# Two of four probability tiles joined on GpSimd at the end of each batch of layer 0

## The reference, cut to what matters

```python
scores2 = jnp.einsum('bqh,bkh->bqk', Q_sub, K_char) * scale
sub2char = jnp.einsum('bqk,bkh->bqh', jax.nn.softmax(scores2, axis=-1), V_char)
sub2char = sub2char[:, lo] * (1 - w) + sub2char[:, hi] * w
gate = jax.nn.sigmoid(jnp.einsum('blh,oh->blo', jnp.concatenate([char2sub, sub2char], -1), Wg) + bg)
x = x + tanh(g_xattn[0]) * (gate * char2sub + (1 - gate) * sub2char)
```

## Time and profile before

| | |
|---|---|
| time of the kernel before | 1392.84 us, median of 3 runs, 1389.47 to 1395.42 |
| span of the profiled execution | 1388.3 us |
| TensorE busy in it | 1323.2 us, 95% |
| VectorE busy | 779.2 us, 56% |
| ScalarE busy | 736.2 us, 53% |
| GpSimd busy | 478.3 us, 34% |
| the gate of batches 0 to 3 ends at | 118.7, 210.8, 302.4 and 392.2 us |

### The profile page before, as it was taken

One profiled execution on the slowest core, in us unless ns is written; L12 is line 12 of the kernel. 1 busy time (PEld: TensorE's weight loads), 2 busy tenths in 40 slices (PEclk: granted clock), 3 DMA queues, 4 the chain that ended last, 5 costly groups with the idle time before them and its releaser, 6 DMA issues. The chain is left out here.

```text
span 1388.3 us, 25467 instructions
## 1 busy us (share of the span) xinstructions
PE 1323.2 (95%) x9828; PEld 1239.0 (89%) x9828; DVE 779.2 (56%) x1736; ACT 736.2 (53%) x1405; POOL 478.3 (34%) x378
## 2 busy tenths in 40 slices
PE   6999999999989999999999998899999999999996
PEld 5987969969759999999998998899999879999996
DVE  6566686776865535435444323666876774466322
ACT  4464555455554655555555554454554546567544
POOL 0100001001026656556465443111201246667544
PEclk9999999999999999999999999999999999999999
DMA  6102031220235545455363334112312166565322
GB/s 225 61 12 92 16 128 46 67 86 7 84 85 159 123 83 148 93 116 146 63 150 54 56 59 88 46 59 70 128 35 92 47 219 159 131 163 127 53 52 40
DMA packets 73675, 127.48 MB, mean 92 GB/s; under 512 B 7952, under 2 KB 53664, under 8 KB 73504
## 3 DMA queue, kind: packets, MB, share of 16 engines
q1 hardware_dynamic: 46816, 81.92, 17.9%
q0 software_dynamic: 26688, 43.34, 16.9%
HBM read 100.44 MB, written 24.79 MB: 90 GB/s over the span
## 5 line engine op out<-in xcount | busy, mean ns | idle before, releaser
L2551 DVE TENSOR_TENSOR m_hidden_lo<-m_act_out,m_hidden_hi 128x512 fp32r<-128x512 f32 x224 | 154.9, 693 | 353.6 <-ACT m_hidden_hi L2491 343.2
L434 PE MATMUL banks<-m_down_hi,m_hidden_hi 128*128 128x256 f32 x896 | 258.5, 288 | 1.4 <-DVE m_hidden_lo L2551 0.9
L434 PE MATMUL banks<-m_down_lo,m_hidden_hi 128*128 128x256 f32 x896 | 255.8, 286 | 2.4 <-issue 2.4
L434 PE MATMUL banks<-m_down_hi,m_hidden_lo 128*128 128x256 f32 x896 | 255.8, 285 | 0.0
L434 PE MATMUL banks<-m_xt_hi,m_up_hi 128*128 128x256 f32 x640 | 184.1, 288 | 1.4 <-DVE m_xt_lo L2534 1.4
L434 PE MATMUL banks<-m_xt_hi,m_up_lo 128*128 128x256 f32 x640 | 180.8, 282 | 0.0
L434 PE MATMUL banks<-m_xt_lo,m_up_hi 128*128 128x256 f32 x640 | 180.6, 282 | 0.0
L434 PEld LDWEIGHTS banks<-m_down_hi,m_hidden_hi 128*128 128x128 f32 x896 | 172.2, 192 | 4.6 <-DVE m_hidden_lo L2551 1.1
L434 PEld LDWEIGHTS banks<-m_down_lo,m_hidden_hi 128*128 128x128 f32 x896 | 172.2, 192 | 2.6 <-issue 2.6
L434 PEld LDWEIGHTS banks<-m_down_hi,m_hidden_lo 128*128 128x128 f32 x896 | 172.0, 192 | 0.0
L2491 ACT ACTIVATE m_hidden_hi<-m_act_out 128x512 fp32r<-128x512 f32 x224 | 141.6, 632 | 7.1
(11 more groups left out here) (387 smaller groups left out, 3430.5 us busy)
## 6 DMA issues: line engine op xcount, KB each, us to landing
stage<-in_up SPq DMA_DIRECT2D x22, 512.0 KB, 5.0
stage<-in_down SPq DMA_DIRECT2D x21, 512.0 KB, 4.0
stage<-in_ctx_rows SPq DMA_DIRECT2D x20, 512.0 KB, 4.3
stage<-in_ctx_cols SPq DMA_DIRECT2D x24, 402.0 KB, 3.3
m_stage<-in_down SPq DMA_DIRECT2D x10, 512.0 KB, 5.2
m_stage<-in_up SPq DMA_DIRECT2D x9, 512.0 KB, 4.8
rows<-xn SPq DMA_DIRECT2D x8, 528.0 KB, 3.7
stage<-in_ctx_picked SPq DMA_DIRECT2D x8, 512.0 KB, 4.6
```

The source lines that it names most:

```text
L434: mm = q.e.matmul(dst, a, b, start=first and n == 0, stop=last and n == 2, skip_group_check=True)
L2551: q.e.tensor_tensor(lo, m.act[(n * HP + h) % ACTS], f32(hi), ALU.subtract).then_inc(*hidden_lo.mark((layer, n, h)))
```

## The change

- **Joins.** Tiles 0 and 1 are joined on GpSimd (`gpsimd_back_finish`): a multiplication of the upper probabilities in place with their weight, and an addition into `a0.pc`. Tiles 2 and 3 stay on VectorE.
- **Sums.** VectorE makes the weights of the upper probabilities one tile at a time, each behind the next tile's scores. ScalarE scales the lower tiles 0, 1, 2 first, then takes the first exponential, then scales tile 3.
- **Turns.** `tensor_turn_pc` takes several blocks: for j = 0 and 1 it takes both banks first, and then for each tile i waits for that tile's join and turns its two blocks. The 6 fillers are gone in batches 0 to 2; the 18 in batch 3 stay.
- **Copies.** ScalarE copies turned blocks 0 and 1 ahead of context piece 0, which now stands with pieces 1 and 2.

```diff
+        def gpsimd_back_finish(q, b, i):
+            src, dst = other_probs(i), a0.pc[:, i, :]
+            q.wait_ge(*back_exped.of("scaled", b, i))
+            q.wait_ge(*back.of("sums", b, 1, i))
+            q.e.tensor_tensor(src, src, rinv2[:, 1, i, 0:1].to_broadcast([P, TOK]), ALU.mult).then_inc(*blended.mark())
+            q.wait_ge(*blended.last())
+            q.e.tensor_tensor(dst, dst, src, ALU.add).then_inc(*blended.mark((b, i)))
+
+        def finished(b, i):
+
+            return blended.of(b, i) if i < 2 else back.of("finish", b, 1, i)
...
         def vector_back_finish(q, b, i):
             dst = a0.pc[:, i, :]
             q.wait_ge(*back_exped.of("scaled", b, i))
-            q.wait_ge(*back.of("sums", b, 1, i - i % 2))
+            q.wait_ge(*back.of("sums", b, 1, i))
...
-        def tensor_turn_pc(q, b, j):
-            use = ("pc", b, j)
-            bank, emptied = gen.take(use, his, use)
-            q.wait_ge(*emptied)
-            if j == 0:
-                stay_busy(q, bank, 6 if b + 1 < BATCH else 18)
-            q.wait_ge(*back.of("finish", b, 1, TT - 1))
+        def tensor_turn_pc(q, b, js):
+            banks = []
+            for j in js:
+                use = ("pc", b, j)
+                bank, emptied = gen.take(use, his, use)
+                q.wait_ge(*emptied)
+                banks.append(bank)
+            if 0 in js and b + 1 == BATCH:
+                stay_busy(q, banks[0], 18)
             for i in range(TT):
-                mm = q.e.transpose(bank[:, i * P:(i + 1) * P], a0.pc[:, i, j * P:(j + 1) * P], ident)
-            mm.then_inc(*turned_pc.mark((b, j)))
+                q.wait_ge(*finished(b, i))
+                for j, bank in zip(js, banks):
+                    mm = q.e.transpose(bank[:, i * P:(i + 1) * P], a0.pc[:, i, j * P:(j + 1) * P], ident)
+                    if i == TT - 1:
+                        mm.then_inc(*turned_pc.mark((b, j)))
...
-                for i in range(TT):
-                    if i % 2 == 0:
-                        scalar_back_scale(q, b, i)
-                        scalar_back_scale(q, b, i + 1)
+                for i in range(TT - 1):
+                    scalar_back_scale(q, b, i)
+                scalar_back_scores(q, b, 1, 0)
+                scalar_back_scale(q, b, TT - 1)
+                for i in range(1, TT):
                     scalar_back_scores(q, b, 1, i)
                 if more:
                     scalar_queries(q, 0, b + 1)
-                convert(q, "a", pieces[0:1])
                 scalar_turn_pc(q, b, 0)
                 scalar_turn_pc(q, b, 1)
-                convert(q, "a", pieces[1:3])
+                convert(q, "a", pieces[0:3])
...
-                for i in range(TT):
+                vector_back_scores(q, b, 1, 0)
+                for i in range(1, TT):
                     vector_back_scores(q, b, 1, i)
-                    if i == 1:
-                        vector_back_sums(q, b, 1, 0, 2)
-                    elif i >= 2:
-                        vector_back_finish(q, b, i - 2)
-                vector_back_sums(q, b, 1, 2, 2)
+                    vector_back_sums(q, b, 1, i - 1, 1)
                 vector_back_finish(q, b, 2)
+                vector_back_sums(q, b, 1, 3, 1)
                 vector_back_finish(q, b, 3)
...
+                gpsimd_back_finish(q, b, 0)
+                gpsimd_back_finish(q, b, 1)
```

More of the change, by code:

```diff
@@ L216, in build @@
         powers, base_out, zeroed = signal("powers"), signal("base_out"), signal("zeroed")
-        applied = signal("applied")
+        applied, blended = signal("applied"), signal("blended")
         rested = signal("rested")
@@ L1788, in tensor_attention_0 @@
                     tensor_put(q, 0, b - 1, 1)
-                tensor_turn_pc(q, b, 0)
-                tensor_turn_pc(q, b, 1)
+                tensor_turn_pc(q, b, (0, 1))
                 for j in range(TT):
@@ L1793, in tensor_attention_0 @@
                     if j + 2 < TT:
-                        tensor_turn_pc(q, b, j + 2)
+                        tensor_turn_pc(q, b, (j + 2,))
                     if j == 1 and b:
```

## The result

| | before | after |
|---|---|---|
| time, median of 6 runs each | 1393.99 us (1389.21 to 1397.24) | 1407.42 us (1404.08 to 1412.41) |
| ratio, 95% interval | | 1.0104, 1.0079 to 1.0129 |
| span of the profiled execution | 1388.3 us | 1410.6 us |

What follows compares the result with a forecast made beforehand. TensorE, busy 95% of the span, was taken as the bound, so only its stops matter. Late chain 9.0, batch 3 0.1 and clock 1.2 make +10.3 us; on a median of 1392.84 that gives 1403 us, range 1394 to 1410.

Steps and rivals of the forecast that it cites:

- The late chain: Ends of batches 0 to 2: piece 0 copied late delays the fetch of piece 3 and mix 2, +3.0 us each.
- The contention: VectorE operations with two SBUF inputs wait for GpSimd's joins, so joining two tiles there gains nothing.
- the last join: VectorE's final join of probabilities in a batch: 0.4 us later than in the kernel before.
- My upper bound, 0.9: Bound on the delay of VectorE's last join in batch 0: at most 0.9 us later.
- Rival (a): VectorE and GpSimd share inputs without contention, last join at 99.82: +2.0 us, 1395 us; chance 0.15.
- The turns: TensorE's turns of both blocks wait for the query bank: start at 102.28 against 101.20, some 0.7 us after the last join.
- Rival (d): TensorE turns nothing as it comes, the bank holds all eight; worth 0.3 to 0.7 us per batch, inside the forecast.
- Batch 3, +0.1: End of batch 3, with no context chain: last join 0.4 us later, ScalarE's copy at 376.2 against 376.14.
- The clock, 0.4 each: TensorE's clock falls without fillers in batches 0 to 2, mostly hidden: 0.4 us per batch, bounds 0 and 1.7.
- the gap before mix 2: Sign of a right forecast: TensorE stands 2 to 3 us before mix 2.
- Rival (b): The clock falls unhidden in mix 2 and the gate, 1.7 us more in three batches: +14.2, 1407 us; chance 0.18.
- Rival (c): Piece 0 is copied in time, no contention arises and TensorE binds: -4.7 us, 1388 us; chance 0.10.

Runs made afterwards that it cites:

- e10: The changed kernel with 14 fillers in batches 0 to 2 ahead of the wait for the second bank; 1413.29 us (before 1400.90 on that chip).
- e1: The kernel before with only ScalarE's copies of turned blocks 0 and 1 moved ahead of context piece 0; 1400.94 us, ratio 1.0048.
- e3: The changed kernel with the one-tile weight taking one SBUF tensor input instead of two; 1403.85 us (before 1393.16 on that chip).
- e7: The changed kernel with block 1 turned into the bank of the second forward value; 1418.78 us (before 1402.41 on that chip).
- e9: The changed kernel with the weight of e3, the bank of e7, the six fillers back and piece 0 early on both engines; 1395.05 us, ratio 0.9948.
- e11: e9 with all four joins on VectorE, none on GpSimd; 1395.73 us (before 1402.41 on that chip).
- e12: e9 with the one-tile weight in its two-input form again; 1401.77 us (before 1402.41 on that chip).
- e8: The kernel before with piece 0 copied early on ScalarE and its low part ahead of the query low parts on VectorE; 1405.15 us, ratio 1.0028.
- e5: The kernel before without its 6 fillers in batches 0 to 2; 1406.92 us (before 1400.90 on that chip).

## Why the prediction was right, and where it was off

The sign and the mechanism were right; the sum was +10.3 us and the medians differ by 13.4, the batch ends by 12.3. The 1403 of the forecast is 4.4 below the 1407.42 measured: 2.0 are terms of the sum that were too low, 1.2 the median of before in this comparison (1393.99), and the last 1.2 lie outside the batch ends.

- **The late chain, +3.0 each.** Right in every link: piece 0 behind the copies, low part 3.3 to 3.8 later, fetch of piece 3, mix 2. e10 gives it without the clock: +3.28 each, 9.8 in all for my 9.0. e1 has the ScalarE order alone at +1.5 each, and e3 takes 1.3 off the changed kernel by one operation.
- **The contention.** L1180 "at about 1 us": 1.18 and 1.15. The term that was mis-sized is the last join, +0.90 for my +0.42. I had taken 1.10 for each operation of GpSimd, from a line through two other shapes; the multiplication took 1.04, the addition 1.29 and 1.26, and its start came 0.13 later than I had it. The held L1180 ends with the addition, so each surplus went straight into the join. My upper bound, 0.9, had it, for another reason. Rival (a) is out: the rows show the hold, and e3 removes it.
- **The turns.** First turn 0.7 after the last join: 0.77. Rival (d) was true as a fact: with the bank of the query ring all eight turns come together in batches 0 to 2; they come tile by tile in batch 3, and in the other batches only with the bank of e7. It was rightly counted inside the forecast.
- **Batch 3, +0.1.** It is +0.57: the same 0.48 of the last join.
- **The clock, 0.4 each, 1.2 in all.** It falls in each of the three batches, in batch 1 for 6.8 us. What is left of 12.3 after 9.8 for the chain and 0.6 for batch 3 is 1.9 us, 0.6 each. (That e10 ends 1.9 below after is no second proof, since the 9.8 come from e10.) The size of 0.4 was low, and its reason, that most is hidden ahead of mix 2, right for the changed kernel. One sign failed by it: the gap before mix 2, 2 to 3 us by forecast, was 1.74, none and 0.91, as the slowed work fills it; with the clock whole, in batch 0 of e10, it is 2.35.
- **Rival (b)** named a time of 1407, and 1407.42 was measured. Its mechanism isn't what happened: the clock fell ahead of mix 2, not in it, and in after's trace mix 2 runs at 3.70 in batch 0, with no low clock during it in batches 1 and 2 either. That the time came so near is luck, made of the three remainders above. The argument against (b), a 9 in every slice of the page of before, was no evidence: that trace has 6.8 us at 0.50 from 416.9 on, and the slice still reads 9; the granted clock over the batch ends themselves is 1.00 there. But e1 and the first batch of e7 show that it is a real case for edits close to this one.
- **Rival (c)**, faster, needed piece 0 in time and no hold. e9 is just that, with the bank and the fillers, and it is faster. The chance of a faster kernel rested on stops of some 12 us at these ends; from +0 to the gate the trace of before has 7.6.

What stays open: why the clock falls in one batch and not in its equal neighbour (e1: batches 0 and 1, not 2; e10: only 2), and, with it, why it was lower behind layer 0 in after's profiled execution, where 6.3 of the 7.9 us are longer busy time of TensorE. No run was made for either.

## What to carry to other kernels

Where a ring of staging slots feeds a later step, the copy that frees a slot is worth more than its own 0.87 us: put it into idle time, ahead of anything that waits for another engine, and then ask which bank or queue its new neighbours hold up. When GpSimd is given work, look at VectorE's smallest operations with two SBUF tensors in that stretch, since each can be held to the end of a GpSimd instruction; the one-tensor form avoids it. On this kernel GpSimd's joins were worth little, 0.5 to 1.1 us per batch (e11), and with the held weight they cost 0.8 instead (batch 0 of e12 against e11, both with the clock whole). Fillers help only ahead of the wait that they are to cover, and an edit that shortens one engine's work can be eaten by a clock that falls in the stop it makes, so judge an edit with the granted clock beside it.

## What the runs showed of the hardware

- A 128x1 VectorE multiplication with two SBUF tensors takes 0.16 us alone and 1.15 to 1.18 beside a GpSimd addition; with a value per partition it takes 0.21 beside the same addition. A 128x512 join that begins during a GpSimd instruction ends 0.55 us after it (0.85 and 1.12 instead of 0.75), and a GpSimd addition that begins during a join ends 1.12 after that (1.59 instead of 1.29).
- GpSimd's 128x512 multiplication of one tensor by a broadcast column takes 1.04 us and its addition of two tensors 1.26 to 1.30.
- The granted clock fell to 0.50 after stops of 3.83, 2.47 and 2.31 us, and also where two stops of 1.23 and 0.91 us had short turns between them (e8, in batches 0 and 1, not in 2), and once behind a stop of 1.50 us that followed fourteen fillers (e10, batch 2). After one stop of 1.23 us behind six fillers it stayed whole in the three batches of before. The length of the stop alone doesn't decide it: e1's batches 1 and 2 have the same work and start mix 2 at the same time to 0.1 us, and only the first of them loses its clock. It stayed at 0.50 for some 3.4 or 6.8 us, with TensorE at work in most of it.
- The price of such a stretch goes from 0.04 us (e5, batch 0) to 1.7 (e1, mix 2 in 5.40 for 3.70), by what waits behind it.
